# First batch of a fused attention block: stacks copied inside SBUF, idle-time turns of the identity

## The reference

```python
xn = layernorm(x)
x_h = xn.reshape(b, t, 16, 16).transpose(0, 2, 1, 3)            # 16 heads of 16
xw  = einsum('bhtd,hde->bhte', x_h, w_att_val)                  # the "queries"
att = softmax(einsum('bhte,bhse->bhts', xw, x_h) / sqrt(16))    # keys are x_h itself
o   = einsum('bhts,bhsd->bhtd', att, (xn @ wv_w.T + wv_b) in heads)
x   = x + o @ out_w.T + out_b
x   = x + ffn(layernorm(x))
```

## Time and profile before

| | us |
|---|---|
| median of 3 runs | 1489.31 (1487.73 to 1489.78) |
| the profiled execution | 1486.98 |
| its span, first to last instruction | 1485.1 |
| all engines leave the first block | about 21.4 |
| first tile of the first pass on TensorE | 25.21 |
| first matmul of the second pass | 46.31 |
| its second step (j = 1) | 56.45 |

### The profile page before, as it was taken

The page is one execution under the profiler, slowest core; times in us unless marked ns, Lnnn a source line. Parts: engine busy times, 40 slices in busy tenths (PEclk is TensorE's granted clock), DMA queues, the critical chain, the costliest instruction groups (busy, mean ns, idle before and its releaser), DMA issues. The chain is left out here.

```text
span 1485.1 us, 32215 instructions
## 1 busy us (share of the span) xinstructions
PE 1422.1 (96%) x8562; PEld 882.9 (59%) x8562; DVE 1267.9 (85%) x2644; ACT 866.0 (58%) x1730; POOL 659.4 (44%) x910
## 2 busy tenths in 40 slices
PE   4699999999999999999999998899999999999998
PEld 2345555555555555555555554577777777777776
DVE  5788888888888888888888887599999999999995
ACT  1477777777777777777777777533333333333332
POOL 2346446446446445445545523234343343434341
PEclk7799999999999999999999999999999999999999
DMA  7655455455456456356356353000000000000000
GB/s 209 192 157 161 133 155 162 124 160 167 122 157 173 119 154 178 111 159 182 106 163 169 103 150 90 1 15 15 18 14 18 14 18 14 18 14 18 14 18 22
DMA packets 99433, 148.09 MB, mean 100 GB/s; under 512 B 20928, under 2 KB 58176, under 8 KB 99392
## 3 DMA queue, kind: packets, MB, share of 16 engines
q1 hardware_dynamic: 82272, 137.08, 32.4%
q10 hardware_dynamic: 17120, 10.51, 2.8%
HBM read 85.02 MB, written 65.27 MB: 101 GB/s over the span
## 5 line engine op out<-in xcount | busy, mean ns | idle before, releaser
L1102 DVE TENSOR_REDUCE neg_max<-ring 128x1 f32<-128x512 f32 x1024 | 642.6, 682 | 107.0 <-PE ring L842 103.3
L991 ACT ACTIVATE probs<-scores 128x512 f32<-128x512 f32 x1024 | 531.2, 602 | 186.2 <-PE scores L853 175.8
L1552 PE MATMUL gu_bank<-splits,f_x_T 128*128 128x352 f32 x1024 | 313.7, 459 | 0.1
L842 PE MATMUL ring<-x_stack,q_stack 64*128 64x512 f32 x1024 | 233.9, 455 | 30.5 <-DVE neg_max L1102 18.8
L875 PE MATMUL ring<-probs,v_quad 128*32 128x512 f32 x2048 | 246.2, 598 | 4.2 <-DVE neg_max L1102 4.1
L1552 PEld LDWEIGHTS gu_bank<-splits,f_x_T 128*128 128x128 f32 x1024 | 189.6, 190 | 95.4 <-ACT f_x_T L1526 0.5
L850 PE MATMUL scores<-q_stack,x_stack 64*128 64x512 f32 x1024 | 206.4, 398 | 4.9 <-DMA max_stack<-max_rows 2.6
L842 PEld LDWEIGHTS ring<-x_stack,q_stack 64*128 64x128 f32 x1024 | 98.3, 188 | 185.7 <-DVE neg_max L1102 138.1
L853 PE MATMUL scores<-max_stack,max_ones 64*128 64x512 f32 x1024 | 203.0, 392 | 0.0
L1308 POOL TENSOR_TENSOR f_small<-f_small,eps 128x1 f32<-128x1 f32 x64 | 43.0, 672 | 295.8 <-DVE f_small L1275 295.8
L649 POOL TENSOR_TENSOR pv_rows<-pv_more,pv_rows 128x512 f32<-128x512 f32 x63 | 80.8, 1283 | 180.8 <-ACT pv_more L997 180.8
(11 more groups left out here) (129 smaller groups left out, 1981.5 us busy)
## 6 DMA issues: line engine op xcount, KB each, us to landing
x_rows<-splits SPq DMA_DIRECT2D x128, 256.0 KB, 3.3
x_stack<-x_rows SPq DMA_DIRECT2D x128, 256.0 KB, 4.0
q_stack<-q_rows SPq DMA_DIRECT2D x248, 128.0 KB, 4.0
q_rows<-splits SPq DMA_DIRECT2D x64, 256.0 KB, 2.2
out_dram<-x_all SPq DMA_DIRECT2D x64, 128.0 KB, 1.7
x_all<-in_L_attn_x_dram ACTq DMA_DIRECT2D x14, 512.0 KB, 4.1
w_raw<-slabs SPq DMA_DIRECT2D x14, 192.0 KB, 3.9
slabs_kept<-w_turned SPq DMA_DIRECT2D x14, 192.0 KB, 3.8
```

Source lines behind the costliest of these rows:

```text
L842: pe.matmul(bank(tiles[m])[:, :], row_tile(q_stack[q], m)[:, p, s * P:(s + 1) * P], row_tile(x_stack[q], m)[:, p, :], start=True, stop=Tru ...
L991: act.activation(probs[j][:, k, :], scores[k][:, :], ACT.Exp).then_inc(p_ready, 1)
L1102: dve.tensor_reduce(neg_max[g % 2][:, at:at + 1], tile[:, :], AX.X, ALU.max, negate=True).then_inc(m_used, 1)
L1552: m = pe.matmul(gu_bank[c][:, :], x_T[u][:, a, :], gate_up_T[:, a, c * CH:(c + 1) * CH], start=(a == 0), stop=(a == HALVES - 1))
```

## The change

Four things are done, all of them in or before the first quads of batch 0.

1. Stacks of quads 0 and 1 of batch 0 are no longer read back from DRAM. `direct_stacks` copies each block of 16 features of one head straight from `splits` to the stack: 16 partitions of 2 KB, taken from every 8th partition. There are 16 such copies for each quad and head pair (g, p), 64 in all, counted by `direct[g][p]`. For (0, 0) SP issues 12 and ScalarE 4, in the first block. In the second block SP issues 16 (x of (0, 1) and (1, 0)), ahead of the stores of half 1; ScalarE's queue issues 32, ahead of `store_maxima(0, 0)`. Half 0 of batch 0 is not stored to DRAM; GpSimd waits until all 64 copies have landed and then raises `stored[0]` by a fill (`half_read`), ahead of `split_maxima(0)`. The load of stack 3 moves behind the wait for `max_loaded[0]`.
2. The first pass of quad 0 uses all 8 PSUM banks (`max_bank`).
3. TensorE turns the identity where it stands idle: 20 times before `turn(0)`, 8 times after it, and 8 times at the start of the second block. Nothing reads these.
4. In the first block: half of the 8 loads of `qw` goes to SP's queue, behind x and ahead of `vw`; batch 0 is normalised by halves of the heads (`normalize_half`), so that TensorE can begin with half 0; VectorE's statistics of batch 1 are moved in between; `raw_first` is replaced by `raw_x`.

```diff
+def direct_stacks(queue, g, p, k, stack, part, direct):
+    a = g * QUAD // HH
+    for m in range(ROWS):
+        h = g * QUAD % HH + PAIRS * m + p
+        queue.dma_start(row_tile(stack[g], m)[D * k:D * k + D, p, :].bitcast(F32), part[h:P:HH, a, :].bitcast(F32))\
+             .then_inc(direct, 16)
...
             load_x(0, 1, x_first)
+            sp.wait_ge(qw_zero, 1)
+            for k in range(HH // 2, HH):
+                load_qw(sp, k)
             sp.dma_start(vw[:, :, :], wv_w.rearrange("(n p) e -> p n e", p=P)).then_inc(vw_loaded, 16)
...
+            sp.wait_ge(xh_done, 1)
+            for k in (0, 3):
+                direct_stacks(sp, 0, 0, k, x_stack, xh, direct[0][0])
             sp.wait_ge(xl_done, 1)
-            store_parts(sp, 0, 0, x_rows, (xh, xl, xl, xh), stored)
+            for k in (1, 2):
+                direct_stacks(sp, 0, 0, k, x_stack, xl, direct[0][0])
             sp.wait_ge(ql_done, 1)
-            store_parts(sp, 0, 0, q_rows, (qh, ql), stored)
+            for k in (1, 3):
+                direct_stacks(sp, 0, 0, k, q_stack, ql, direct[0][0])
             sp.wait_ge(bias_loaded, 32)
-            sp.wait_ge(stored[0], STORES)
-            load_x_stack(sp, 0, 0, x_stack, x_rows, stack_loaded)
...
                 act.activation(qh[:, a, :], q_bank[a][:, :], ACT.Copy, scale=D ** -0.5).then_inc(qh_done, 1)
+                if a == 0:
+                    act.wait_ge(qh_done, 1)
+                    for k in (0, 2):
+                        direct_stacks(act, 0, 0, k, q_stack, qh, direct[0][0])
             move(1)
-            act.wait_ge(stored[0], STORES)
-            load_q_stack(act, 0, 0, q_stack, q_rows, stack_loaded)
...
+            def warm(n):
+                for _ in range(n):
+                    pe.transpose(v_bank[0][:, 0, 0:P], ident[:, :], ident[:, :])
...
             pe.wait_ge(ident_made, 1)
+            warm(20)
             turn(0)
+            warm(8)
             for a in range(HALVES):
-                pe.wait_ge(xn_done, TT)
+                pe.wait_ge(x_half_done if a == 0 else xn_done, TT)
...
-            normalize(0)
-
+            normalize_half(0, x_half_done)
+            normalize_half(1, xn_done)
             dve.wait_ge(qw_loaded, 16 * HH)
...
+            dve.wait_ge(x_second, 16)
+            statistics(1, range(2))
             low_x(0)
+            statistics(1, range(2, TT))
             low_x(1)
+            aggregate(1)
             low_q(0)
-            dve.wait_ge(x_second, 16)
-            statistics(1)
             low_q(1)
-            aggregate(1)
             normalize(1)
...
+    def max_bank(c, q, k):
+        if isinstance(c, int) and c == 0 and q == 0:
+            return (*ring, *scores)[k % 8]
+        return bank(("max", (q - 2) % QUADS, k))
...
+            def half_read():
+                for g in range(DIRECT):
+                    for p in range(PAIRS):
+                        pool.wait_ge(direct[g][p], 2 * PARTS)
+                pool.memset(w_turned[:, P:], 0.0).then_inc(stored[0], STORES)
...
             pool.wait_ge(pool_set, set_up())
+            half_read()
             split_maxima(0, 0, True)
...
-            load_x_stack(sp, 0, 1, x_stack, x_rows, stack_loaded)
+            direct_x(sp, 0, 1)
+            direct_x(sp, 1, 0)
             store_parts(sp, 0, 1, x_rows, (xh, xl, xl, xh), stored)
             store_parts(sp, 0, 1, q_rows, (qh, ql), stored)
-            for g in range(2, QUADS):
-                load_stacks(sp, 0, g, x_stack, q_stack, x_rows, q_rows, stored, stack_loaded)
+            load_stacks(sp, 0, 2, x_stack, q_stack, x_rows, q_rows, stored, stack_loaded)
             sp.wait_ge(max_loaded[0], 16 * ROWS)
+            load_stacks(sp, 0, 3, x_stack, q_stack, x_rows, q_rows, stored, stack_loaded)
             copy_weights()
...
+            for _ in range(8):
+                pe.transpose(scores[-1][:, 0:P], ident[:, :], ident[:, :])
             for g in range(2):
                 for n in range(PAIRS * TT):
...
-            load_q_stack(act, 0, 1, q_stack, q_rows, stack_loaded)
+            direct_q(act, 0, 1)
+            direct_q(act, 1, 0)
+            direct_q(act, 1, 1)
+            direct_x(act, 1, 1)
             store_maxima(0, 0)
             load_maxima(0, 0)
```

## The result

| | before | after |
|---|---|---|
| median, us (4 runs each) | 1488.52 (1487.56 to 1489.78) | 1494.94 (1494.59 to 1497.55) |
| ratio, 95% interval | | 1.0047 (1.0032 to 1.0062) |
| profiled execution, and its span | 1486.98, 1485.1 | 1494.94, 1492.7 |
| first tile of the first pass | 25.21 | 23.25 |
| last reduction of quad 0 ends | 37.42 | 33.92 |

A forecast was written before the change was run, and what follows sets the result against it. TensorE sets the pace after about 60 us, so an earlier second pass counts: maxima turned at 37.5 plus a 6.5 trip gives 44.0 instead of 46.31. Thus 1489.3 - 2.3 = 1487.0, stated as 1486.9, range 1482.5 to 1492.0.

The forecast's parts named there:

- I take 0.38 with the gap: Second block, ScalarE's queue: each of 32 copies issues in 0.38 us, the last at 34.4, landed at 36.6.
- the rival: Copies issue at 0.66 us like `qw`; ScalarE's 32 end at 44.4, second pass at 53 to 54, 1496; chance 0.17.
- the 0.45 at which the change gains nothing: Copies on ScalarE's queue: from an issue pitch of 0.45 us on, no gain; at 0.54 a cost of 3 us.
- the slow issue: The same case as the rival: copies issue at 0.66 us, 7 us late; chance 0.17, centre 1493.5.
- the split of the maxima released by a DMA and not by VectorE: Sign ahead of the second pass: GpSimd's split waits for copies, VectorE idle 2 us between its 16th and 17th reduction.
- no cost from the late stack 3: Stack 3, issued at 44 and landed near 52, is needed about 14 us after stack 2, so it is covered.
- The two-step chain: Ahead of the second pass: `half_read` holds the maxima and VectorE's later reductions; the maxima's store queues behind ScalarE's 32 copies.
- The landing: End of the 64 copies: 2.2 us from the last issue at 34.4 to landed at 36.6.
- The trip of the maxima: From turned maxima through DRAM to the second pass: 6.5 us instead of 7.97, bounds 5.5 and 7.97.
- full clock from the start: Profile page's reading of the clock; the prediction took the low level, 1.2 GHz, to hold until some time before 14.7.
- low-clock times: First block and turns: summed at the low clock level, such as 8 idle turns at 0.25 us each.
- The third case: The clock stays up through the first pass, 2.7 us together, giving 1484.2; chance 0.18.

The follow-up runs named there:

- e2: The changed kernel with three of four copies reading adjacent, every 2nd or every 4th partition instead of every 8th; issue medians 0.611 or 0.612 us, run time not compared.
- e8: The changed kernel with some later copies replaced by 16-row stores to DRAM or 32-row copies inside SBUF, little traffic; run time not compared.
- e6: The changed kernel with only quad 0 copied directly, quad 1 through DRAM, no wait for copies, all `qw` on ScalarE's queue; 1483.86, ratio 0.9970 to the kernel before.
- e10: e6 with no direct copy at all, all stacks of batch 0 through DRAM; 1484.76, ratio 0.9983 to the kernel before.
- e1: The changed kernel with GpSimd's wait for the 64 copies moved behind `split_maxima(0)`; 1491.74, ratio 1.0023 to the kernel before.
- e9: The kernel before with only stack 3's load moved behind the wait for `max_loaded[0]`; 1485.07, ratio 0.9979 to the kernel before.
- e7: The kernel before with 8 banks for quad 0's first pass and stack 3's load behind the wait for `max_loaded[0]`; 1484.52, ratio 0.9977.
- e3: The changed kernel without its 36 turns of the identity; 1497.71, ratio 1.0064 to the kernel before.
- e12: The same kernel as e6, run on a second occasion; 1483.61, ratio 0.9966 to the kernel before.
- e5: The changed kernel with copies behind those for (0, 0) replaced by transfers of 16 to 128 rows, inside SBUF and to DRAM; run time not compared.
- e11: e6 without its 36 turns of the identity; 1484.36, ratio 0.9972 to the kernel before.

## Why the prediction was wrong

**The step that failed** is the term "I take 0.38 with the gap" for the issue of one copy. It measured 0.67 with the gap. The rest of that step, put right, gives 21.8 + 32 x 0.67 = 43.3 for the last issue (34.4 in the prediction, 44.4 by the rival), and the copy had landed by 47.95 (36.6, and 46.6 by the rival). Two rows stood for choice, 0.37 for transfers with long rows between SBUF and DRAM and 0.66 for `qw`. I chose by row length and named the stride as what spoke for the dear one. The stride does not decide (e2). The rows of the copies were as long as those of the cheap transfers, 2 KB, and that did not make them cheap. What the cheap transfers lack is SBUF at both ends, which e8 leaves standing and does not prove. `qw` comes out of DRAM too, so that its 0.66 was near the right price is luck as far as the runs show.

Nearer neighbours stood in the trace and were passed over. The 0.37 is a median over the whole run, most of it the loop. Between 17.9 and 25.4 us the kernel before issues these, ScalarE's own queue among them:
```profile
L172 ACTq DMA_DIRECT2D q_stack<-q_rows x8: 337/462/599, 17.9 to 22.9; - x8
L184 SPq DMA_DIRECT2D x_rows<-splits x4: 432/500/578, 22.7 to 24.3; - x4
```
With gaps of 0.03 to 0.04 that is about 0.49 and 0.54, both dearer than the 0.45 at which the change gains nothing. They were issued beside more traffic than the copies had, so they don't give the copies' price, but they would have moved the centre.

The Trainium skill, page "DMA: Bandwidth & Descriptors", Rules for kernel authors, spoke against copies of 32 KB, as transfers under 64 KB pay mostly overhead. The trace agrees in that each took 0.6 us of a queue; but quad 0's 32 copies alone brought the second pass 1.9 us forward (e6 against e10), so what decided is how many of them stood ahead of the maxima.

The break-even lay at 0.45, so with 0.25 to 0.66 as bounds half of the interval was on the slow side; a chance of 0.17 for the slow issue was too low, and the range, which cut off its dear half, was too narrow.

**Right**, each by its row: `vw_dh` 7.17 (7.7), `xn` 9.64 (10.3), the block's end 21.8 (22.1), the first tile 23.25 (23.9), the 16 reductions 9.8 us with 8 banks (9.9), their end 33.9 (34.6), the split of the maxima released by a DMA and not by VectorE, the same window from 200 to 500 us, and no cost from the late stack 3. The clock came back at 66.7 and not at 57, but 2.5 us behind the second step, as before. The two-step chain, that `half_read` holds VectorE's whole program and that the store queues behind the copies, is shown by e1: with the first link cut, the second pass comes 5.5 us earlier, and the second link keeps it 2.4 us later than before.

**The landing** was 2.2 in the sum, counted from the issue's end. From an issue's start the median of all copies is 2.0 us and the longest 5.1, which is the last one's; from its issue's end to GpSimd's fill it was 4.6 us (43.33 to 47.95), while stack 2's loads, issued at 38.98 to 42.8, were in flight (DMA share 0.76 from 43.0 to 47.5). These 2.4 us too much were in no case of the prediction, the rival's neither.

**The trip of the maxima** was put at 6.5 and took 5.2, since no stack load was in flight by then. That the old trip was long because of the stack loads is shown by e9: store to load 5.8 us before and 2.1 with stack 3 held back, nothing else changed. The other traces say when. Where a stack's loads were still in flight 2.1 us behind the store, the load of the maxima issued within 0.6 us of their landing: 5.8 us behind the store before, 4.0 in e7, 3.6 in e10, 3.4 in e1. In e6, with stores to DRAM in flight and no loads, it was 2.1. The changed kernel had the shorter trip, by 2.7 us, which is why turning the maxima 10.6 us late made the second pass only 7.9 late; the gain of the banks was hidden behind the copies. The late stack 3 alone, in the kernel before, is worth 0.2%.

**The clock.** It rose at 5.3 us, fell at 8.7, and rose at 12.1; then it fell at 22.3, rose at 25.7 and fell at 29.2, and came back to stay at 66.7. Windows that end before the first rise print 1.00 too, although the turns there took 421 ns: the record of the clock begins with the rise, and the prediction's "full clock from the start" was this. Windows of the kernel after at some of those places (9 to 10 is the low level, 26 to 27 the high one):
```profile
9.00:10.00 1.00, 1.00 (x7) 1.00 (x6) 0.36 (x2) 0.60 (x1) 0.60 (x1) 0.50 1.08 370
...
26.00:27.00 1.00, 0.00 (x0) 0.00 (x0) 1.00 (x2) 0.00 (x0) 0.77 (x5) 1.00 0.34 99
...
66.00:67.00 1.00, 1.00 (x8) 0.50 (x4) 0.41 (x1) 1.00 (x3) 0.00 (x0) 0.65 0.88 212
```
The prediction took low-clock times for the first block; in fact the queries ran at the high level, 2.01 us instead of the 3.6 without turns (e3), which made up for the four copies that ScalarE issues between the two `qh` (2.60 us, where the sum had 1.5). That the block's end was met is in part luck, two errors that cancel; the first `qh` came at 14.05 and not at 15.4 to 16.1. The third case, a clock that stays up through the first pass, did not come about: TensorE waited 3.2 us for copies at 25.3 to 28.5.

**Where the best version's gain comes from**, at the second pass: stack 3 late, 46.31 to 43.43 (e9); banks, to 42.23 (e7); the first block's other parts, nothing (42.27, e10); quad 0's copies, to 40.34 (e6). That is 6.0 us, but only 4.0 to 4.1 arrive in the medians, where the last two steps are not resolved. The first exponential (`probs`) starts at 41.4 in both traces of that kernel; the last starts at 938.7 in e6 and 937.1 in e12, against 47.5 and 941.9 before. The second steps of e6 and e12 begin at 50.34 and 50.35, and the clock comes back at 58.2 in one and 52.8 in the other, where TensorE sets the pace. So one kernel differs by 1.6 us from one execution to the next with 5.4 us more at the low level behind the second step. Over all fourteen traces, from the second step to the last exponential takes 887.9 to 888.8 us in the five where the clock came back 7.9 to 9.0 us behind the second step (e2, e5, e6, e10, e11), and 884.0 to 887.1 in the nine where it came back within 3.9. So a late return fits as the cause of part of the loss. It was not tried by itself, and the 3 us of spread among the nine have no cause here.

## What to carry to other kernels

Before work is put on a queue, multiply its issues by the price of the dearest neighbour, not of the likeliest, and read neighbours in the same stretch and not over the whole run, if anything on the critical path is queued behind them or waits for their last; where no row has both ends in the same memories, the price is unknown and the forecast must be that wide. A wait in an in-order program has to stand behind the work that does not need it. When a small transfer is on the critical path, hold the bulk loads back until it is through: by the medians one moved load gave 2.9 of the best version's 4.0 us (e9).

## What the hardware showed that was not expected

- A copy from SBUF to SBUF takes 0.59 us to issue on SP's queue and 0.61 on ScalarE's, for 16 or 32 rows of 2 KB and for any stride tried. A store of 16 rows to DRAM behind another such takes 0.41 to 0.47 (e8), behind a copy 0.57 to 0.60.
- The clock rose during twenty turns of the identity, with nothing else on TensorE before. Durations of them, minimum, median and maximum in ns, up to 4 us and from 5 us on:

```profile
L335 PE MATMUL v_tiles<-ident x12: 421/421/473, 1.6 to 4.0; 128*128 128x128 f32 x12
L335 PE MATMUL v_tiles<-ident x4: 272/275/381, 5.0 to 5.5; 128*128 128x128 f32 x4
```

  They get shorter, 421 to 272 ns, at the place where the granted clock goes to 2.4 GHz (5.3 us). In the nine traces with the turns the clock rose at 4.8 to 11.1 us, in the five without them at 12.9 to 17.4. The Trainium skill, page "TensorE: Matmul & The Clock Gate", Part 4 (PE-mode transpose), says that transposes do not count; this trace does not agree, as far as these turns ran in the mode that the page means: the trace records them as fp32 matmuls.
- A store of 16 KB and its semaphore take 2.1 us with no stack load in flight and 5.8 us beside 2 MB of stack loads (store's issue to the next load's issue).
